# Filler matmuls of 192 columns behind every flock of the swept recurrence, and streaming matmuls through its check, the adding of states and the next norm

## The reference

```python
def _L0_ffn_ref(x, W, V, gamma, beta):     # x: [2, 1024, 32]
    Wx = jnp.einsum('bti,hi->bth', x, W)
    flat = Wx.reshape(B * T, H)
    mean, var = jnp.mean(flat, axis=0), jnp.var(flat, axis=0)
    Wx = ((flat - mean) * jax.lax.rsqrt(var + BN_EPS) * gamma + beta).reshape(B, T, H)
    def step(yt, wx_t):
        yt = jax.nn.sigmoid(wx_t + yt @ V.T)
        return (yt, yt)
    _, ys = jax.lax.scan(step, y0, jnp.swapaxes(Wx, 0, 1))
    return jnp.swapaxes(ys, 0, 1)
...
t = t + _L0_ffn_ref(_ln_t(t), ...)          # the states are added to the residual
x = x + _L1_conv_ref(_ln_c(x), ...)         # begins with a norm over the channels
```

## Time and profile before

| | |
|---|---|
| three runs, us | 1003.05, 1003.53, 1009.89; median 1003.53 |
| span of the profiled execution, us | 1000.8 |
| swept recurrence, first to last flock matmul (L944) | 318.1 to 353.8 |
| norm of layer 1's mixer, first transpose to last copy | 359.7 to 366.3 |
| TensorE's granted clock, mean over the span | 0.942 |
| PE busy, share of the span | 87% |

### The profile page before, as it was taken

One profiled execution on the slowest core, in us unless ns is written; L12 is line 12 of the kernel. 1 busy time (PEld: TensorE's weight loads), 2 busy tenths in 40 slices (PEclk: granted clock), 3 DMA queues, 4 the chain that ended last, 5 costly groups with the idle time before them and its releaser, 6 DMA issues. The chain is left out here.

```text
span 1000.8 us, 13608 instructions
## 1 busy us (share of the span) xinstructions
PE 871.9 (87%) x5288; PEld 440.0 (44%) x5363; DVE 424.3 (42%) x723; ACT 448.7 (45%) x1486; POOL 226.7 (23%) x136
## 2 busy tenths in 40 slices
PE   7849878788885877889999999999999999999886
PEld 4413333333343534344444444445555544555543
DVE  4599999999955744610000000002104500202763
ACT  4667767776725543233333333333333333333642
POOL 3009999898910000020000000000000000000410
PEclk9968999999997569699999999999999999999987
DMA  3020000000000000020000000000000000000000
GB/s 74 17 48 0 1 0 1 0 1 0 1 0 7 1 1 24 13 78 1 1 1 1 1 1 1 1 1 1 1 1 1 1 1 1 1 1 1 2 24 11
DMA packets 10314, 8.05 MB, mean 8 GB/s; under 512 B 7475, under 2 KB 8611, under 8 KB 10153
## 3 DMA queue, kind: packets, MB, share of 16 engines
q1 hardware_dynamic: 10248, 7.18, 3.0%
HBM read 5.34 MB, written 0.26 MB: 6 GB/s over the span
## 5 line engine op out<-in xcount | busy, mean ns | idle before, releaser
L852 PE MATMUL L2p_z<-stream 128*128 128x512 bf16 x880 | 342.6, 390 | 0.0
L894 ACT ACTIVATE L2yx<-L2p_z 32x2 f32<-32x2 f32 x1024 | 165.0, 161 | 323.3 <-PE L2p_z L871 323.3
L871 PE MATMUL L2p_z<-L2yx,L2v 64*32 64x2 f32 x2048 | 225.5, 178 | 16.9 <-ACT L2yx L894 15.9
L871 PEld LDWEIGHTS L2p_z<-L2yx,L2v 64*32 64x32 f32 x2048 | 137.6, 104 | 224.5 <-ACT L2yx L894 218.3
L632 POOL TENSOR_TENSOR hc<-hs,cb 128x1024 f32<-128x1024 f32 x64 | 149.4, 2353 | 17.9 <-DVE hs L612 17.9
L1550 DVE COPY xn<-L2yx 32x512 f32<-32x512 f32 (+1 forms) x2 | 0.8, 385 | 302.7 <-ACT L2yx L894 302.7
L556 PE MATMUL p_y<-hc,ident 128*128 128x512 f32 x256 | 123.0, 603 | 5.1 <-DVE y_seq L595 2.8
L612 DVE TENSOR_TENSOR_SCAN hs<-d_a,p_bb 128x1024 f32<-128x1024 f32 x48 | 109.8, 2287 | 6.3
L1550 POOL COPY xn<-L2yx 32x128 f32<-32x128 f32 x1 | 0.3, 283 | 484.2 <-SPq L1893 484.2
L852 PEld LDWEIGHTS L2p_z<-stream 128*128 128x128 bf16 x943 | 90.2, 96 | 15.1
L556 PEld LDWEIGHTS p_y<-hc,ident 128*128 128x128 f32 x256 | 47.7, 192 | 50.5 <-issue 31.3
(11 more groups left out here) (501 smaller groups left out, 852.4 us busy)
## 6 DMA issues: line engine op xcount, KB each, us to landing
y_seq<-in_pick SPq DMA_DIRECT2D x1, 768.0 KB
b_parts<-part SPq DMA_DIRECT2D x6, 128.0 KB, 2.3
c_parts<-part SPq DMA_DIRECT2D x6, 128.0 KB, 2.3
pos<-in_pos SPq DMA_DIRECT2D x1, 512.0 KB, 3.7
ao<-in_at_o SPq DMA_DIRECT2D x1, 512.0 KB, 4.2
L1w<-in_L_w SPq DMA_DIRECT2D x1, 297.0 KB
L3w<-in_L_w SPq DMA_DIRECT2D x1, 297.0 KB
x_tok<-in_x SPq DMA_DIRECT2D x2, 128.0 KB, 3.0
```

The costliest lines, as they stand in the source:

```text
L852: pe.matmul(p_z[:, 1, 0:each], stream[:, 0:128], stream[:, 0:each], start=True, stop=True)
L871: pe.matmul(p_step[:, t % 2], v[:, 0:C], yx[:, NB * t:NB * (t + 1)], start=True, stop=True).then_inc(s("preact"), 1)
L894: act.activation(yx[0:C, NB * (t + 1):NB * (t + 2)], p_step[:, t % 2], ACT.Sigmoid).then_inc(s("state"), 1)
```

## The change

Three things are put in, and nothing is taken out. Behind each flock's matmul stands a filler of 192 columns (128 x 128 weights, bf16) from `stream`, 96 in all. In the check, 3 streaming matmuls of 512 columns stand ahead of the summing matmul and 2 behind it. In the block that adds the states, TensorE streams 11 matmuls of 512 columns, and the next norm has 11 streaming matmuls in place of 7. Their results go to PSUM banks of their own (`p_fill`, `p_moving`) or the norm's old one, and nobody reads them.

```diff
@@ recurrent, swept @@
                     p_g = ps(tag + "p_g", [R, BANK], stack=s2)
+                    p_fill = ps(tag + "p_fill", [128, BANK], stack=s2)
+                    BESIDE = 192
...
                                     pe.matmul(p_z[0:C, f, 0:NB * n], v[:, 0:C], by_batch[:, cols], start=True, stop=True).then_inc(s("preact"), 1)
+                                    pe.matmul(p_fill[:, 0:BESIDE], stream[:, 0:128], stream[:, 0:BESIDE], start=True, stop=True)
+                            keep_streaming(pe, p_fill[:], 3)
                             pe.wait_ge(s("differ"), 1)
                             pe.matmul(p_f[:, 0:1], ones64[0:C, 0:C], count[:], start=True, stop=True).then_inc(s("differs"), 1)
+                            keep_streaming(pe, p_fill[:], 2)
                             pe.wait_ge(s("flag"), 1)
...
+            p_moving = ps(tag + "p_moving", [128, BANK], stack=st)
             with nc.Block() as block:
+                @block.tensor
+                def _(pe):
+                    keep_streaming(pe, p_moving[:], 11)
...
@@ mixer of layer 1 @@
             def _(pe):
-                norm.pe(pe, 7)
+                norm.pe(pe, 11)
```

## The result

| | before | after |
|---|---|---|
| median of 4 runs each, us | 1003.34 | 1029.51 |
| lowest to highest | 1003.05 to 1009.89 | 1028.91 to 1030.65 |
| span of the profiled execution | 1000.8 | 1027.1 |

The ratio is 1.0256, with an interval of 1.0226 to 1.0287: slower by 26 us. From the start of the first flock's matmul to the end of the next norm the two traces take 48.20 and 73.62 us, +25.4; of the other +0.9 of the span, −0.8 lies ahead of the sweeps and +1.7 in later stages.

A forecast was written before the change was run, and what follows sets the result against it. The sweeps were bound by flock 0's own loop, TensorE waiting for ScalarE's sigmoid. Steps +26.0, lag +0.4, L1059 +0.2, check +0.5, adding +2.0 and norm -1.1 gave +28.0, a time of 1031.5 us, range 1020 to 1038.

The forecast's parts named there:

- The sign and the mechanism: Sweeps: slower, as two weight-shape changes per flock make TensorE the bound, steps 1.30 us against 0.735, +26.0 us.
- the way back, 0.14: Sweeps: the change from the filler's weight shape back to the flock's costs 0.14 us at the half clock.
- the lower bound: Sweeps: at 0.62 us per flock a step takes 1.24 us, and the steps cost +23.2 us.
- L1059's +0.2: End of the sweeps: the matmul of L1059 gets two dearer neighbours, +0.2 us.
- The tail: Behind the steps: later last flock 1 +0.4, check +0.5, adding of states +2.0, next norm -1.1 us.
- lag and check: End of the sweeps: flock 1 of the last step starts later, +0.4 us, and the check's matmul waits, +0.5 us.
- adding: Block adding the states: eleven matmuls at the half clock outlast VectorE's adds, +2.0 us (bounds +1.0 to +2.3).
- norm: Next norm, behind the adding block: runs at the full clock after so much streaming, -1.1 us (bounds -1.2 and 0).
- The clock: Sweeps: stays at 1.2 GHz until after the last flock, with columns streaming 58% of a step against 60% before.
- The first: Rival, sweeps: fillers bring the clock up in the first sweep, steps 0.78 us, +2.1 us, time 1004.5; chance 0.10.
- The second: Rival, sweeps: shape changes cost nothing, the clock rises, the loop sets 0.58 us, -7.1 us, time 995.2; chance 0.03.

The follow-up runs named there:

- e1: The changed kernel with its fillers' weights 64 x 32, the flocks' own shape, and the same 192 columns: 1008.0 us against 1003.88, ratio 1.0042.
- e6: The changed kernel with filler weights of 64 x 128 in rows 64 to 127, which the flocks don't use: 1030.47 us against 1004.69.
- e7: The changed kernel with fillers of 32 columns in place of 192, weights still 128 x 128: 1018.27 us against 1004.69.
- e11: The changed kernel with flocks zero-filled to 128 x 32 and 128 x 32 fillers of 192 columns: 998.62 us against 1003.74, ratio 0.9951.
- e2: The changed kernel plus 22 streaming matmuls ahead of the sweeps and 4 behind the first step: 1028.12 us against 1003.88, ratio 1.0247.
- e10: The changed kernel with zero-filled 128 x 32 flocks, 128 x 32 fillers and streaming ahead of the sweeps: 997.98 us against 1002.47, ratio 0.9951.
- e9: The changed kernel with 64 x 32 fillers of 448 columns and streaming ahead of the sweeps to bring the clock up: 999.64 us against 1002.47.
- e5: The changed kernel with 64 x 32 fillers of 192 columns and streaming ahead of the sweeps to bring the clock up: 1011.23 us against 1004.69.
- e8: The changed kernel with 128 x 128 fillers of 512 columns and streaming ahead of the sweeps to bring the clock up: 1018.24 us against 1004.69.

## Why the prediction was right, by its steps

**The sign and the mechanism held.** The flock and its filler hold TensorE longer than the loop allows, because of two changes of shape; the wait for the sigmoid is gone from the changed trace, and e1 takes the changes away and gets the step back to 0.74. That the price is one of shape, and not of number format or of shared rows, was assumed. e6 excludes the rows. As to the format, have the price between two fp32 matmuls, and e1 has none between bf16 and fp32. Nor is it the size of the filler's weights alone: the flock's small weights, behind the filler, come 0.11 late as well.

**The mis-sized term is the way back, 0.14.** It was taken between 0.13 and 0.17, both from the step with L1059. It measured 0.11, so a flock costs 0.62 in place of 0.65, a step 1.24 in place of 1.30, the lower bound, and the 46 intervals +23.6 (1.250 less 0.736 each) in place of +26.0 and L1059's +0.2. Between the two profiled spans the forecast is only 1.7 too high (28.0 against 26.3), for 0.9 that was not foreseen (below) went the other way; that part of the nearness is luck. The 0.13 was the way to another shape, not back from it. Why 0.17 passed behind L1059 stays open: its short stream of 30 columns is not the reason, since e7 has about 0.10 behind 32.

The Trainium skill has two rules here. One (TensorE: Matmul & The Clock Gate, "Step-by-step: what each phase is for") has weights pulled ahead of a matmul in flight when the row groups don't conflict or the load goes to the background buffer. In e1, whose fillers use the flocks' own rows, they come ahead of the end of the stream (341.32), so there it can only be the second case. In e6, whose fillers use other rows, they come 0.13 behind the end of the stream (340.49): for two shapes the first case did not hold. The other (TensorEngine Tiling (Array Packing), "Key Properties") has a change of the tiling mode, and not of the tile alone, drain the engine. The traces agree: 0.11 to 0.13 us pass at each change in the changed kernel, and none in e1.

**The tail held:** lag and check +0.9 as forecast, adding +1.9 for +2.0, norm −1.0 for −1.1. The check's sum stands 23.8 us later (355.06 to 378.81) and not about 27: 2.6 for the step's size, 0.8 because the sweeps began earlier.

**The clock was forecast right for a reason that does not carry.** The argument was that columns stream for 58% of a step against 60% before. e1 streams with hardly a pause and still has 0.50, and e11 has the same columns and comes up. So the share of streaming time could not have told which way it goes, and that it told rightly here is luck. The Trainium skill (TensorE: Matmul & The Clock Gate, "What's actually happening") has the clock follow how busy the engine has been. e11's trace agrees, with PE busy for 4.44 of 4.50 us and 1.00 behind it; e1's does not as far as the profile's busy time goes, 35.14 of 35.50 us at 0.50.

**The rivals.** The first needed fillers that bring the clock up; in e2 fillers of 192 columns did not even hold it, and a step at 1.00 was 0.82, not 0.78. The second had the right cure for the wrong kernel: with shapes alike the changes cost nothing and the loop at the full clock is 0.60 (0.58 was worked out), but the runs show 1.00 throughout the sweeps only with all rows filled (e10; from the seventh step behind the first in e11) or with 448 columns (e9), and not with 192 columns of 64 x 32 (e1, e5). Its 995.2 is 3 us under what e10 reached.

**Not foreseen:** −0.8 ahead of the sweeps and +1.7 behind the norm. They are differences between single executions. Of the 1.7, layer 1's later block takes +3.0 (24.3 to 27.3 us, at a granted clock of 0.76 in place of 0.91) and the block behind it −1.6 (18.2 to 16.6, at 0.78 in place of 0.65). So the clock stood low at other times; why stays open. So does why filling the rows matters to the clock; the runs show that it does, not how it is weighed, nor whether the flocks' zeros or the fillers' further ones do it.

## What to carry to other kernels

A filler between small matmuls is priced first by its weights' shape: make it that of the work around it, and it slips into the wait; with another shape it costs twice a change, at either clock. Then see in a trace whether it moves the clock at all, since in e1 TensorE was busy nearly all the time and the clock stayed down. Where the work uses half of the array's rows, filling them up cost the steps nothing here (the work's own with zeros, the fillers' with ones), and with both done the clock rose.

## What the runs showed of the hardware that was not expected

- The change of weight shape costs 0.13 us there and 0.11 back at 1.2 GHz; with fillers of 64 x 128 in other rows than the flocks' as much; with 64 x 32 in both, in bf16 and fp32, nothing that the timeline shows.
- The clock stayed at 0.50 for 35 us under a TensorE busy 99% of the time with weights over 64 rows (e1), and rose six steps behind the first, in the same rhythm, with weights over 128 rows, half of the flocks' being zeros (e11).
- Brought up, it fell five to seven steps behind the first with fillers of 192 columns of 128 x 128 and of 64 x 32, and stayed up with 512 and 448 of these (e2, e5, e8, e9).
